# A table of PSUM banks, an output projection for two tiles, whole-tile turns and values, and another order of stages in the layers of a transformer kernel

## The chip, the core and the metric

The kernel runs on one core of a Trainium2 chip. Its engines work side by side, each through its own list of instructions in order: TensorE (PE; matmuls, with their weight loads as PEld), VectorE (DVE), ScalarE (ACT) and GpSimd (POOL); SyncE (SP) issues the DMAs. They wait for each other on semaphores. Matmul results land in PSUM, eight banks of 128 partitions x 512 float32 values; everything else lies in SBUF. The metric is the device time of one execution in microseconds (us), lower is better.

## What is computed

Two branches read the same normalised input of 2048 tokens x 128 features; their results and the input are added.

```python
xn = _layernorm(x)
x = x + _L0_attn_ref(xn, ...) + _L0_ffn_ref(xn, ...)

# dense attention: 16 heads of 8, softmax over all 2048 tokens, values, output projection
# the layers, DEPTH = 6, HEADS = 16, DIM_HEAD = 64, WINDOW = 32:
for i in range(DEPTH):
    x = attn_layer(shift_tokens(x), Wqkv[i], q_scale[i], k_scale[i], Wo[i]) + x
    x = ffn_layer(shift_tokens(x), ln_g[i], ln_b[i], W1[i], b1[i], W2[i], b2[i]) + x

def attn_layer(x, Wqkv, qs, ksc, Wo):
    q, k, v = heads of x @ Wqkv
    q, k = l2norm(q) * qs, l2norm(k) * ksc
    q, k = rotary of both: t * cos * scale + rotate_half(t) * sin * scale
    out = local_attention(q, k, v)      # windows of 32 see themselves and the 32 before
    return out @ Wo

def ffn_layer(x, g, bln, W1, b1, W2, b2):
    xn = layer norm of x, * g + bln
    a, gate = split(xn @ W1 + b1)
    return a * gelu(gate) @ W2 + b2
```

## The kernel before

The program has two stages. The first (functions ending in `_a`, about the first 800 us) does the dense attention; the change doesn't touch it. The second (ending in `_b`) does the six layers and ends with the sum of both branches.

The layers work on **tiles** of 128 tokens, 16 a layer, 96 in all, and on **chunks** of four tiles (512 tokens) for the MLP, 24 in all. Each engine has one loop `for u in range(FIRST, LAST)` in which it calls its stages, each for a tile or chunk that lies some steps back: `tile(u - 2)` is tile u-2 if there is one, `chunk(u - 5)` is a chunk in every fourth step only. The order of the calls in these loops is the order of the engine's instructions; it is written out by hand. A **step** here is one turn of the loop, one tile; four steps make a group with one chunk's MLP work.

The life of a tile: ScalarE rounds the input to its upper part (`high_x`), GpSimd makes the rest (`low_x`); TensorE projects q, k, v (`project`, six matmuls each into two banks); ScalarE squares q and k (`squares`), VectorE sums them (`square_sums`, `root_argument`), ScalarE takes logarithm, exponential and square (`root_estimate`), VectorE corrects the root (`root_slope`, `root_fix`) and scales (`normalise`). q is rotated by VectorE (`rotate_cos`, `rotate_sin`) and summed by GpSimd (`rotate_q_sum`); k is rotated and summed by GpSimd (`rotate_k_cos`, `rotate_k_sin`, `rotate_k_sum`). TensorE transposes both (`turn`), ScalarE evicts them (`turned_q`, `turned_k`, which also makes the 32 columns that the next tile sees). Then `score` on TensorE, `maxima` and `shifted` on VectorE, `exponentials` on ScalarE, `prob_sums` and `prob_reciprocals` on VectorE, `scale_probs` on GpSimd, `blocks` (a transposition in blocks of 32) on VectorE, `diagonals` (eight copies of 32 partitions) on ScalarE, `values` on TensorE, `values_out` on ScalarE, `output` on TensorE, `residual_1` on VectorE.

A chunk: `mean`, `deviation`, `deviation_squares`, `variance`, `add_epsilon`, `ln_root_estimate`, `first_scale`, `ln_root_slope`, `ln_root_fix`, `high_ln`, `scale_shift`, `low_ln`, three `up_product`s, three `gelu`s between two table loads of ScalarE, three `gated`, `down_product`, `residual_2`.

PSUM in the layers: `W_ps` is two pairs of banks for the projections and up products, `SB_ps` a pair for the scores, `T_ps` two single banks for all the rest. Who has which bank is counted in `bank_turns`: users take the two in turn, in the order of TensorE's list, so each waits until the last but one has been evicted. A tile's turn of q is four transposes into one `T_ps` bank and four into the other (halves `hf`), its values likewise; ScalarE evicts a half of 512 columns at a time.

```python
def turned_q(u, hf):
    w.wait_ge(s[f"turn0{hf}"], u + 1)
    w.wait_ge(s["score_mm"], u)
    e.activation(m.q_T[:, 4 * hf:4 * hf + 4, :], bank, ACT.Copy)...
```

## Time and profile before

| | us |
|---|---|
| median of 3 runs | 2631.66 (2623.95 to 2635.92) |
| the profiled execution | 2620.41 |
| its span, first to last instruction | 2618.6 |
| TensorE busy | 2284.9 (87%) |
| VectorE busy | 2249.0 (86%) |
| ScalarE busy | 2025.8 (77%) |
| GpSimd busy | 1327.1 (51%) |

The page says how long each engine was busy, in 40 slices of the span how busy it was, and it follows the chain of work that ended last: 40% TensorE, 29% VectorE, 24% ScalarE, 5% issue. In the dense stage (the first third) the chain is TensorE's almost alone; in the layers it changes engine every few instructions. The granted clock of TensorE is 0.952 of full speed in the mean. DMA carries 37 GB/s and is no limit. Below, a row of a timeline gives the start, the length and, in brackets, how long the engine was idle before it and who released it. Line numbers are those of the kernel before.

### The profile page before, as it was taken

To read this page: it belongs to the slowest core of one execution; us is meant where nothing else is said; L and a number is where in the kernel's file an instruction comes from. 1 tells how busy PE (TensorE), PEld (TensorE's weight loads), DVE (VectorE), ACT (ScalarE), POOL (GpSimd) and SP (SyncE) were. 2 spreads that over 40 slices of the span, in tenths; PEclk is the share of its full clock that TensorE was granted. 3 is DMA by queue.
4 is the path that set the end of the run, shared out by engine and by line. 5 is a ranking of instruction groups with operands and counts; after the bars stand their busy time and mean duration, and the time that the engine had idled before them with its cause. 6 is when DMAs were issued, how large, how long until landed. Compare 5 with 4: busy or idle time off the path is not lost.

```text
span 2618.6 us, 67512 instructions
## 1 busy us (share of the span) xinstructions
PE 2284.9 (87%) x28055; PEld 1393.2 (53%) x28151; DVE 2249.0 (86%) x2609; ACT 2025.8 (77%) x3616; POOL 1327.1 (51%) x894
## 2 busy tenths in 40 slices
PE   5899999999985898888988888888898998889886
PEld 3122222222213676666766666666676766666664
DVE  6999899999926889988889888888888888889984
ACT  1288787778873678888888888888888888888774
POOL 4111111101005567677676676677776666677660
PEclk8699999999997789999999999999999999999998
DMA  1212222222111100100011100101010000111000
GB/s 38 83 50 87 63 84 66 81 51 51 35 61 43 36 18 8 58 18 24 10 40 34 25 10 8 58 16 26 10 56 18 23 10 8 58 26 30 22 14 9
DMA packets 115173, 95.94 MB, mean 37 GB/s; under 512 B 72118, under 2 KB 89780, under 8 KB 114868
## 3 DMA queue, kind: packets, MB, share of 16 engines
q1 hardware_dynamic: 114516, 91.42, 12.7%
q8 instruction: 222, 3.64, 0.6%
q14 instruction: 83, 0.68, 0.1%
q10 hardware_dynamic: 352, 0.20, 0.0%
HBM read 57.83 MB, written 27.26 MB: 32 GB/s over the span
## 4 chain that ended last, share of the span: by engine, by line
PE 40%; DVE 29%; ACT 24%; issue 5%; POOL 1%; DMA 0%; ACTq 0%; DVEq 0%; SPq 0%; POOLq 0%
PE O_ps L1260 9%; PE E_ps L1252 8%; DVE ss L959 6%; PE S_ps L1243 5%; DVE mx L915 4%; ACT nrm L677 4%; DVE nrm L987 3%; ACT pT L746 3%; DVE mxB L1043 3%; PE W_ps L1284 3%; DVE tc L998 2%; PE T_ps L1402 2%; ACT pT L748 2%; PE W_ps L1286 2%; PE W_ps L1285 2%
## 5 line engine op out<-in xcount | busy, mean ns | idle before, releaser
L666 ACT ACTIVATE PT<-E_ps 128x512 f32<-128x512 f32 x1024 | 534.3, 602 | 186.8 <-PE E_ps L1252 185.1
L915 DVE TENSOR_REDUCE mx<-S_ps 128x1 f32<-128x1024 f32 x512 | 601.2, 1218 | 30.8 <-PE S_ps L1243 25.2
L1309 PE MATMUL T_ps<-ident,tc 128*128 128x128 f32 x1536 | 240.1, 289 | 174.1 <-ACT q_T L697 144.0
L608 POOL TENSOR_TENSOR tc<-tc,ts 128x1024 f32<-128x1024 f32 x96 | 228.2, 2377 | 289.5 <-DVE ts L1011 289.5
L1243 PE MATMUL S_ps<-KS,QS 48*128 48x512 bf16 x1024 | 326.8, 403 | 30.3 <-DVE mx L915 22.0
L1252 PE MATMUL E_ps<-QS,KS 64*128 64x512 bf16 x1024 | 318.0, 387 | 4.7 <-ACT PT L666 4.6
L543 POOL CAST w_cut_b<-w_raw_b 128x512 fp32r<-128x512 f32 (+1 forms) x48 | 27.6, 574 | 555.8 <-DMA w_raw_b<-in_Wqkv 417.1
L566 POOL TENSOR_TENSOR pr<-pr,mxB 128x1024 f32<-128x1024 f32 x96 | 182.7, 1903 | 223.8 <-DVE mxB L1050 223.8
L1309 PEld LDWEIGHTS T_ps<-ident,tc 128*128 128x128 f32 x1536 | 175.1, 145 | 221.4 <-ACT q_T L697 109.9
L1284 PE MATMUL W_ps<-w_qkv,x_cut 128*128 128x512 f32 x576 | 272.1, 472 | 23.6 <-issue 15.3
L959 DVE TENSOR_REDUCE ss<-nrm 128x16 f32<-128x1024 f32 x192 | 233.0, 1214 | 68.4 <-ACT nrm L677 66.6
L1260 PE MATMUL O_ps<-PT,va 128*32 128x512 f32 x2048 | 278.3, 616 | 0.0
L746 ACT ACTIVATE pT<-pc 32x512 f32<-32x512 f32 x384 | 240.0, 625 | 16.3 <-DVE pc L1023 9.6
L1252 PEld LDWEIGHTS E_ps<-QS,KS 64*128 64x128 bf16 x1024 | 78.8, 94 | 320.1 <-ACT PT L666 235.1
L677 ACT ACTIVATE nrm<-W_ps 128x1024 f32<-128x1024 f32 x192 | 193.1, 1006 | 58.7 <-PE W_ps L1286 58.7
L1323 PE MATMUL T_ps<-pT,v 128*64 128x128 f32 x3072 | 221.0, 288 | 19.1 <-ACT xl L817 6.4
L1285 PE MATMUL W_ps<-w_qkv,x_cut 128*128 128x512 f32 x576 | 235.2, 408 | 0.0
L1286 PE MATMUL W_ps<-w_qkv,x_cut 128*128 128x512 f32 x576 | 234.9, 408 | 0.0
L616 POOL TENSOR_TENSOR tc<-tc,ts 128x1024 f32<-128x1024 f32 x96 | 227.6, 2370 | 13.8
L588 POOL TENSOR_TENSOR tc<-nrm,rt 128x1024 f32<-128x1024 f32 x96 | 231.4, 2411 | 2.9 <-DVE nrm L987 2.9
L987 DVE TENSOR_TENSOR nrm<-W_ps,rs 128x1024 f32<-128x1024 f32 x192 | 221.9, 1197 | 0.1
L998 DVE TENSOR_TENSOR tc<-nrm,rt 128x1024 f32<-128x1024 f32 x96 | 210.3, 2191 | 0.0
(199 smaller groups left out, 4739.5 us busy)
## 6 DMA issues: line engine op xcount, KB each, us to landing
Wqkv_cut<-w_cut_b SPq DMA_DIRECT2D x72, 256.0 KB, 2.4
w_qkv<-Wqkv_cut SPq DMA_DIRECT2D x36, 512.0 KB, 4.7
rot<-in_rot SPq DMA_DIRECT2D x96, 128.0 KB, 2.5
w_raw_b<-in_Wqkv SPq DMA_DIRECT2D x36, 256.0 KB, 3.0
W_cut<-w_cut_b SPq DMA_DIRECT2D x24, 170.5 KB, 2.6
w<-W_cut SPq DMA_DIRECT2D x12, 341.0 KB
QS<-zp_q SPq DMA_DIRECT2D x96, 32.0 KB
w_o<-in_Wo SPq DMA_DIRECT2D x6, 512.0 KB, 4.0
```

The costliest lines, as they stand in the source:

```text
L666: e.activation(m.PT[n % NPT][:, :], turns.bank("probs", n)[:, :], ACT.Exp).then_inc(turns.sem("probs", n), 1)
L677: e.activation(m.nrms[u % 2][i][:, :].rearrange("p (a b) -> p a b", a=2), turns.w_bank("qk"[i], u)[:, :, :], ACT.Square).then_inc(s[f"sq{i ...
L746: e.activation(m.pT[r, :, r], m.pc[r, :, WIN:2 * WIN], ACT.Copy).then_inc(s["pD"], 1)
L915: e.tensor_reduce(m.mx[h % 2][:, i, hf:hf + 1], m.S_ps[n % 2][:, :, :], AX.XY, ALU.max).then_inc(s["sc_max"], 1)
L959: e.tensor_reduce(m.ss[u % 2][:, i * H:(i + 1) * H], view(m.nrms[u % 2][i][:, :]), AX.X, ALU.add).then_inc(s[f"ss{i}"], 1)
L987: e.tensor_tensor(view(m.nrms[u % 2][i][:, :]), bank[:, :, :].rearrange("p a (h d) -> p (a h) d", d=DH), m.rs[u % 2][2][:, i * H:(i + 1) * ...
L1243: mm = e.matmul(m.S_ps[n % 2][:, c, :], m.QS[sl][rows, i * P:(i + 1) * P], m.KS[sl][rows, k:k + CH], start=True, stop=True)
L1252: e.matmul(turns.bank("probs", n)[:, :], m.KS[sl][rows, j * P:(j + 1) * P], m.QS[sl][rows, chunk_cols(c)], start=True, stop=True).then_inc ...
L1260: e.matmul(m.O_ps[VC * c:VC * (c + 1), :], m.va[:, j, h, :], m.PT[n % NPT][:, :], start=(j == 0), stop=(j == NT - 1)).then_inc(s["pv"], 1)
L1284: e.matmul(bank, left[0], right[0], start=True, stop=False)
L1285: e.matmul(bank, left[0], right[1], start=False, stop=False)
L1309: t = e.transpose(bank[:, j, :], m.tcs[u % 2][i][:, b * P:(b + 1) * P], m.ident[:, :])
```

## The change

It touches the second stage alone.

- **Banks by a table.** PSUM is four pairs of banks, `ps[0]` to `ps[3]` (banks 0 to 7). `BANKS` gives each stage its bank or pair, for even and odd units. `bank_users` goes through TensorE's order and notes, for each use, the last user of each of its banks; `wait_free` waits for that user's eviction. The four counting semaphores `W_out`, `T_out` become one for each stage.
- **Whole tiles.** A turn is eight transposes into a pair of banks and one eviction of 1024 columns; so are the values. `turned_k` has one copy of 256 columns for the next tile in place of two of 128.
- **Output for two tiles.** `o_T` holds two tiles, `output` is eight matmuls of 256 columns in every second step, `residual_1` two additions of 256 columns.
- **The scores** alternate between two pairs of banks.
- **Order.** All five engines' loops are in another order and with other distances. In the diff `tile(u - 2)` for ScalarE stands for the tile that VectorE has at `u`.
- **Small.** `rotate_sin` no longer waits for `rotate_cos`; `squares` waits for `rotq_c`/`rotk_c` too; the buffers of the last addition are single; the weights of the next layer are loaded one tile later.

Of the loops of ScalarE, VectorE and TensorE the diff is shown without its removed lines, which stand in the kernel above.

```diff
-def bank_turns():
+BANKS = {"q": ((0, 1), (0, 1)), "k": ((2, 3), (2, 3)), "v": ((6, 7), (6, 7)),
+         "q_turn": ((6, 7), (6, 7)), "k_turn": ((4, 5), (4, 5)), "values": ((4, 5), (4, 5)),
+         "output": ((0,), (2,)), "score": ((6, 7), (4, 5)), "mean": ((6,), (6,)),
+         "var": ((2,), (2,)), "up0": ((4, 5), (4, 5)), "up1": ((2, 3), (2, 3)),
+         "up2": ((6, 7), (6, 7)), "down": ((5,), (3,)), "att": ((5,), (3,)),
...
+    def take(stage, unit):
         if unit is not None:
-            book[(name, unit) + rest] = len(book) + 1
+            of = BANKS[stage][unit % 2]
+            users[stage, unit] = [last[b] for b in of if b in last]
+            last.update({b: (stage, unit) for b in of})
...
+    def wait_free(self, w, stage, unit):
+        for had, n in self.m.users[stage, unit]:
+            w.wait_ge(self.s[OUT[had]], n + 1 - (CHUNKS - NC if had == "finish" else 0))
...
 def gpsimd_b(e, w, m, s):
...
     for u in range(FIRST, LAST):
-        scale_probs(tile(u - 4))
-        low_x(tile(u - 1))
-        rotate_k_cos(tile(u - 2))
-        rotate_q_sum(tile(u - 2))
-        rotate_k_sin(tile(u - 2))
-        rotate_k_sum(tile(u - 2))
         rotary(tile(u))
+        low_x(tile(u))
+        scale_probs(tile(u - 3))
+        rotate_k_cos(tile(u - 1))
+        rotate_q_sum(tile(u - 1))
+        rotate_k_sin(tile(u - 1))
+        rotate_k_sum(tile(u - 1))
...
 def scalar_b(e, w, m, s):
...
     for u in range(FIRST, LAST):
+        squares(tile(u - 2), 0)
+        squares(tile(u - 2), 1)
+        deviation_squares(chunk(u - 6))
+        high_ln(chunk(u - 7))
+        exponentials(tile(u - 4))
+        root_estimate(tile(u - 2))
+        values_out(tile(u - 5))
+        scale_shift(chunk(u - 7))
+        dense_output(early(u - 5))
+        turned_q(tile(u - 3))
+        turned_k(tile(u - 3))
         high_x(tile(u))
+        keep_v(tile(u - 2))
+        ln_root_estimate(chunk(u - 6))
+        gelu_table(chunk(u - 7))
+        gelu(chunk(u - 7), 0)
+        gelu(chunk(u - 7), 1)
+        diagonals(tile(u - 4), 3)
+        diagonals(tile(u - 4), 2)
+        diagonals(tile(u - 4), 1)
+        diagonals(tile(u - 4), 0)
+        gelu(chunk(u - 7), 2)
+        root_table(chunk(u - 7))
...
 def vector_b(e, w, m, s):
...
     for u in range(FIRST, LAST):
+        ln_root_fix(chunk(u - 5))
         maxima(tile(u - 2))
+        shifted(tile(u - 2))
         gated(chunk(u - 6), 2)
         square_sums(tile(u), 0)
+        deviation(chunk(u - 4))
         square_sums(tile(u), 1)
         root_argument(tile(u))
+        prob_sums(tile(u - 2))
+        low_ln(chunk(u - 5))
         root_slope(tile(u))
+        prob_reciprocals(tile(u - 2))
         root_fix(tile(u))
         normalise(tile(u), 1)
         dense_norm(early(u - 2))
+        normalise(tile(u), 0)
+        add_epsilon(chunk(u - 4))
+        blocks(tile(u - 2))
+        gated(chunk(u - 5), 0)
+        rotate_cos(tile(u))
+        first_scale(chunk(u - 4))
+        ln_root_slope(chunk(u - 4))
+        rotate_sin(tile(u))
+        final_add(late(u - 7))
+        residual_1(pair(u - 3))
+        gated(chunk(u - 5), 1)
+        residual_2(chunk(u - 6))
+        final_sum(late(u - 6))
...
 def tensor_b(e, w, m, s):
...
     for u in range(FIRST, LAST):
+        turn(tile(u - 2), 1)
         project(tile(u - 1), 2)
         up_product(chunk(u - 6), 0)
+        up_product(chunk(u - 6), 1)
+        down_product(chunk(u - 7))
         up_product(chunk(u - 6), 2)
+        finish(late(u - 8))
+        output(pair(u - 4))
+        variance(chunk(u - 5))
         score(tile(u - 2))
         project(tile(u), 0)
+        mean(chunk(u - 4))
         project(tile(u), 1)
+        values(tile(u - 3))
         dense_output(early(u - 3))
+        turn(tile(u - 1), 0)
```

Below, names are those of the tiles: `ss` is a sum of squares, `rs` the roots, `mxB` maxima, sums and reciprocals, `nrm` normalised q or k, `tc` and `ts` the cosine and sine products, `pc` the transposed blocks, `pr` the probabilities.

VectorE in a plain step, from the first `square_sums` to the sine product, before:

```order
L959 TENSOR_REDUCE ss<-nrm 128x16
L1043 TENSOR_REDUCE mxB<-pr 128x16
L959 TENSOR_REDUCE ss<-nrm 128x16
L966 TENSOR_SCALAR rs<-ss 128x32
L973 SCALAR_TENSOR_TENSOR rs<-rs 128x32
L980 SCALAR_TENSOR_TENSOR rs<-rs 128x32
L1050 RECIPROCAL mxB<-mxB 128x16
L987 TENSOR_TENSOR nrm<-W_ps,rs 128x1024 x2
L1023 STREAM_TRANSPOSE pc<-pr 128x1024
L998 TENSOR_TENSOR tc<-nrm,rt 128x1024
L1009 TENSOR_TENSOR ts<-nrm,rt 128x16x32
```

And after:

```order
L956 TENSOR_REDUCE ss<-nrm 128x16 x2
L963 TENSOR_SCALAR rs<-ss 128x32
L1037 TENSOR_REDUCE mxB<-pr 128x16
L970 SCALAR_TENSOR_TENSOR rs<-rs 128x32
L1044 RECIPROCAL mxB<-mxB 128x16
L977 SCALAR_TENSOR_TENSOR rs<-rs 128x32
L983 TENSOR_TENSOR nrm<-B_ps,rs 128x1024 x2
L1017 STREAM_TRANSPOSE pc<-pr 128x1024
L993 TENSOR_TENSOR tc<-nrm,rt 128x1024
L1003 TENSOR_TENSOR ts<-nrm,rt 128x16x32
L1005 TENSOR_TENSOR ts<-nrm,rt 128x16x32
```

The sums of the probabilities (`mxB<-pr`) moved from between the two sums of squares to behind `root_argument` (`rs<-ss`), the reciprocals before `root_fix`.

GpSimd in the same step, before, from `scale_probs` on (`pr<-pr,mxB`):

```order
L566 TENSOR_TENSOR pr<-pr,mxB 128x1024
L559 TENSOR_TENSOR x_cut<-stream,x_cut 128x128
L588 TENSOR_TENSOR tc<-nrm,rt 128x1024
L608 TENSOR_TENSOR tc<-tc,ts 128x1024
L598 TENSOR_TENSOR ts<-nrm,rt 128x16x32
L600 TENSOR_TENSOR ts<-nrm,rt 128x16x32
L616 TENSOR_TENSOR tc<-tc,ts 128x1024
L579 TENSOR_TENSOR rt<-rot,gains 128x256
```

And after:

```order
L565 TENSOR_TENSOR pr<-pr,mxB 128x1024
L586 TENSOR_TENSOR tc<-nrm,rt 128x1024
L606 TENSOR_TENSOR tc<-tc,ts 128x1024
L596 TENSOR_TENSOR ts<-nrm,rt 128x16x32
L598 TENSOR_TENSOR ts<-nrm,rt 128x16x32
L614 TENSOR_TENSOR tc<-tc,ts 128x1024
L578 TENSOR_TENSOR rt<-rot,gains 128x256
L558 TENSOR_TENSOR x_cut<-stream,x_cut 128x128
```

`low_x` (`x_cut`) moved from behind `scale_probs` to ahead of it; the rest of the row is as it was.

TensorE at the end of a step, before (turns are `ident,tc`, values `pT,v` and `pL,v`):

```order
L1309 MATMUL T_ps<-ident,tc 128x128 x4
L1323 MATMUL T_ps<-pT,v 64x128 x8
L1329 MATMUL T_ps<-pL,v 64x32 x8
L1309 MATMUL T_ps<-ident,tc 128x128 x4
L1323 MATMUL T_ps<-pT,v 64x128 x8
L1329 MATMUL T_ps<-pL,v 64x32 x8
L1309 MATMUL T_ps<-ident,tc 128x128 x8
```

And after, with the beginning of the next step:

```order
L1314 MATMUL B_ps<-pT,v 64x128 x16
L1320 MATMUL B_ps<-pL,v 64x32 x16
L1301 MATMUL B_ps<-ident,tc 128x128 x16
L1276 MATMUL B_ps<-w_qkv,x_cut 128x512
L1277 MATMUL B_ps<-w_qkv,x_cut 128x512
L1278 MATMUL B_ps<-w_qkv,x_cut 128x512
L1276 MATMUL B_ps<-w_qkv,x_cut 128x512
L1277 MATMUL B_ps<-w_qkv,x_cut 128x512
L1278 MATMUL B_ps<-w_qkv,x_cut 128x512
L1351 MATMUL B_ps<-o_T,w_o 128x256 x8
L1334 MATMUL B_ps<-mask_bf,ident_bf 128x512 x2
L1339 MATMUL B_ps<-k_T,q_T 32x64 x64
```

The values of a tile are in one piece, then q's turn, k's turn of the tile before it (together the row of 16), v's projection, the pair's output, the scores.

## Rows read from the trace of the kernel before

**Rows 1.** Busy times by stretch: start:end, length, engines (instructions), PEclk, DMA share, GB/s.

```profile
1600.00:2400.00 800.00, 709.90 (x10890) 547.90 (x10932) 702.83 (x869) 674.50 (x1177) 552.04 (x353) 0.97 0.10 27
```

**Rows 2.** `maxima` (L1029): its summary, then timeline rows of VectorE (start, us).

```profile
L1029 DVE TENSOR_REDUCE mxB<-SB_ps x96: 1214/1218/1226, 826.6 to 2565.8; 128x16 f32<-128x1024 f32 x96
...
1870.39 1.22 DVE L1029 TENSOR_REDUCE mxB<-SB_ps 128x16 f32<-128x1024 f32 x1
...
1886.50 1.22 DVE L1029 TENSOR_REDUCE mxB<-SB_ps 128x16 f32<-128x1024 f32 x1
...
1906.47 1.22 DVE L1029 TENSOR_REDUCE mxB<-SB_ps 128x16 f32<-128x1024 f32 x1
...
1924.92 1.22 DVE L1029 TENSOR_REDUCE mxB<-SB_ps 128x16 f32<-128x1024 f32 x1
```

**Rows 3.** Groups of instructions, 1600 to 2400 us: busy, mean ns | idle before, releasers.

```profile
L1309 PE MATMUL T_ps<-ident,tc 128*128 128x128 f32 x704 | 108.0, 286 | 76.9 <-ACT q_T L697 70.1 <-POOL tc L608 3.1 <-ACT o_T L719 3.1
```

**Rows 4.** Timeline of VectorE, one step, 1937 to 1951 us.

```profile
1937.99 2.51 DVE L998 TENSOR_TENSOR tc<-nrm,rt 128x1024 f32<-128x1024 f32 x1
1940.61 0.69 DVE L1009 TENSOR_TENSOR ts<-nrm,rt 128x512 f32<-128x512 f32 x1
...
1941.83 1.22 DVE L1029 TENSOR_REDUCE mxB<-SB_ps 128x16 f32<-128x1024 f32 x1
...
1948.38 1.01 DVE L966 TENSOR_SCALAR rs<-ss 128x32 f32<-128x32 f32 x1
1950.20 0.19 DVE L973 SCALAR_TENSOR_TENSOR rs<-rs 128x32 f32<-128x32 f32 x1 [0.82 <-ACT rs L689]
```

**Rows 5.** Timeline of GpSimd, the same step.

```profile
1934.77 1.90 POOL L566 TENSOR_TENSOR pr<-pr,mxB 128x1024 f32<-128x1024 f32 x1 [1.63 <-DVE mxB L1050]
...
1937.05 2.38 POOL L588 TENSOR_TENSOR tc<-nrm,rt 128x1024 f32<-128x1024 f32 x1
1941.99 2.40 POOL L608 TENSOR_TENSOR tc<-tc,ts 128x1024 f32<-128x1024 f32 x1 [2.56 <-DVE ts L1011]
...
1946.99 2.36 POOL L616 TENSOR_TENSOR tc<-tc,ts 128x1024 f32<-128x1024 f32 x1
...
1950.86 1.90 POOL L566 TENSOR_TENSOR pr<-pr,mxB 128x1024 f32<-128x1024 f32 x1 [0.83 <-DVE mxB L1050]
```

**Rows 6.** Groups of instructions, 1600 to 2400 us, ScalarE and VectorE.

```profile
L746 ACT ACTIVATE pT<-pc 32x512 f32<-32x512 f32 x176 | 110.0, 625 | 3.1
...
L697 ACT ACTIVATE q_T<-T_ps 128x512 f32<-128x512 f32 x88 | 51.2, 582 | 0.0
...
L734 ACT ACTIVATE v<-W_ps 128x1024 f32<-128x1024 f32 x44 | 45.2, 1028 | 18.1 <-PE W_ps L1286 17.7
...
L810 ACT ACTIVATE gel<-W_ps,b 128x512 f32<-128x512 f32 x22 | 15.1, 687 | 6.0 <-PE W_ps L1286 5.9
L795 ACT ACT_TABLE_LOAD x11 | 14.1, 1283 | 0.2
...
L791 ACT ACTIVATE xl<-xl,cols 128x512 f32<-128x512 f32 x11 | 8.8, 803 | 0.0
...
L1079 DVE TENSOR_SCALAR lnv<-T_ps 128x512 f32<-128x512 f32 x11 | 7.6, 692 | 2.9 <-PE T_ps L1381 2.4
```

**Rows 7.** Timelines of TensorE, then ScalarE, 1934 to 1940 us.

```profile
1934.71 1.07 PE L1309 MATMUL T_ps<-ident,tc 128*128 128x128 f32 x8 [0.41 <-ACT q_T L697]
1935.85 0.50 PE L1284 MATMUL W_ps<-w_qkv,x_cut 128*128 128x512 f32 x1
...
1939.30 2.05 PE L1364 MATMUL T_ps<-o_T,w_o 128*128 128x128 f32 x16
...
1937.55 1.02 ACT L734 ACTIVATE v<-W_ps 128x1024 f32<-128x1024 f32 x1 [0.38 <-PE W_ps L1286]
```

**Rows 8.** TensorE's timeline at 1602 us, then busy times and clock at 1604 us.

```profile
1602.20 0.66 PE L1309 MATMUL T_ps<-ident,tc 128*128 128x128 f32 x4 [1.89 <-ACT q_T L697]
...
1604.00:1605.00 1.00, 1.00 (x18) 0.93 (x16) 1.00 (x4) 0.81 (x1) 0.56 (x1) 0.50 0.00 0
```

441 lines of the change are left out of this document (183 added, 258 removed).

## The prediction

> **What bounds the kernel now.** I read four views, in this order. The busy times of a long stretch of the layers say that no engine is full: in 800 us TensorE is busy 710, VectorE 703, ScalarE 675, GpSimd 552 [rows 1]. So a dependency cycle sets the step, not one engine's sum. The rows of `maxima` give the step: 96 of them between 826.6 and 2565.8 us, 95 steps at 18.31 us; a regular group of four steps takes 16.11, 19.97, 18.45 and 16.91, together 71.44 us (17.86 a step) [rows 2]. The difference, 0.45 us a step or 43 us in all, is what disturbed groups cost.
>
> Among the waits the change speaks to one: in these 800 us TensorE's turns wait 70.1 us for the eviction of q_T [rows 3]. But the timelines of one step show who ends last. VectorE works back to back from one `maxima` to the next, but for the 0.82 us in which `root_slope` waits for ScalarE's roots, and for two instructions that are long without having more work: the cosine product took 2.51 us and ended as GpSimd's cosine product of k (1937.05 + 2.38) was over plus about 1.1, and the tiny `root_argument` took 1.01 us and ended with GpSimd's sum of k (1946.99 + 2.36 = 1949.35) [rows 4, 5]. An instruction of VectorE that reads only SBUF thus stands still while a GpSimd instruction runs. I call this the lock. GpSimd in turn waits 2.56 us for the sine product and 0.83 us for the reciprocals [rows 5]. VectorE and GpSimd hold each other in one cycle; TensorE's wait for an eviction, 1.89 us at its longest here [rows 8], lies beside it.
>
> The Trainium skill, GPSIMD Engine Reference, section 1 (Specifications), says that GpSimd shares its SBUF interfaces with VectorE and contends with VectorE instructions in a 2-port mode or with two SBUF inputs. It gives no price and doesn't say that the one waits for the other's end; if contention only slowed the two a little, the new step would be the 15.2 us of the first rival.
>
> **ScalarE and TensorE, the visible part.** Two evictions of 512 columns (2 x 0.582) become one of 1024 (1.028 in the nearest row, v) [rows 6]: 0.14 less for each of q_T, k_T and o_T. The two carry copies of 128 columns become one of 256; between nothing and 0.58 less (the 512-column eviction is the upper bound), I take 0.3. Together 0.7 us a tile of ScalarE. The output product has the same columns in half the instructions: 16 passes of 128 columns take 2.05 us [rows 7], a pair's 16 passes of 256 should take 3.5 to 4.1, so between 0.1 more and 0.3 less a tile. The turns no longer wait for each other's banks, which frees up to 70.1/44 = 1.6 us a step of TensorE. None of this is on the cycle of VectorE and GpSimd. Cost or gain on the path: nothing, as long as the path through them stays shorter than the new step. It is: roots 0.82, eviction of o_T 1.03, then k's turn and v's projection up to v's eviction (1937.55 - 1934.71 = 2.84), x_cut and v 1.3 (between one and two evictions; x_cut is 128 columns), eight copies of 0.625 = 5.0, two squares of 1.0 each, a sum of 1.2, some 0.3 of handoffs: 14.5 us [rows 4, 6, 7].
>
> **The plain step.** Take the start of GpSimd's `scale_probs` as zero. Before, the sum of k ended at 1949.35 - 1934.77 = 14.58 [rows 5]. In the new order `low_x` no longer stands between `scale_probs` and the cosine product of k (1937.05 - 1934.77 - 1.90 = 0.38 less), and the removed wait of the sine product on the cosine product frees 0.11 (1937.99 + 2.51 to 1940.61) [rows 4, 5]: 14.1. VectorE gets there: the normalisations and the block transposition end at 3.5, the cosine product must wait for the lock till 4.3 and ends as before. Next, `root_argument`. It is ready 14.5 us after the last one, that is 1.2 us before the step is over, and GpSimd's sum of k has then been running since 11.7: it waits for the lock until 14.1. Then come the sums of the probabilities (moved between argument and slope, 1.2 us, which hides the 0.82 us of roots), slope 0.1 and reciprocals 0.3: the next `scale_probs` starts at **15.7**. GpSimd itself would be ready at 14.1 + 0.7 (`rotary`, from 1949.35 to 1950.86 - 0.83) + 0.4 (`low_x`) = 15.2. So the gain of hiding the roots is eaten by the sums put in their place.
>
> **The three steps with the MLP's work.** Times again from `scale_probs`, in the order of tiles 2 to 5 of a group.
> - Into the step with `deviation`: TensorE has the pair's output product (3.5) and, new, the two passes of `mean` (half of the 2.05 in rows 7, since the columns are) ahead of k's projection. Squares and sum come 1.0 us later each, `root_argument` is ready at 14.9, just behind the sum of k, and is held by `low_x` till 15.1: 15.1 + 1.7 = **16.8** (before 16.1).
> - With `add_epsilon`: it waits for the variance product, which stands behind k's turn and v's projection (about 3.9 instead of 2.3); blocks 1.2, cosine 1.1, two operations of 0.6 and the sines 1.2 bring q's sine to 9.3 instead of 6.7, and `ln_root_fix` may go ahead of GpSimd's sum in the lock (0 to 0.69, I take 0.5). The sum of k, 7.4 behind q's sine as in the plain step, ends at 17.2. Then `low_ln`, now ahead of `root_slope`, waits for ScalarE's roots 0.8, o_T 0.9 and `scale_shift` 0.8, which the same `root_argument` held, and takes 0.6 (each to the start of the next, 0.1 less than its length); with slope and reciprocals 17.2 + 0.8 + 0.9 + 0.8 + 0.6 + 0.4 = **20.7** [rows 6] (before 20.0).
> - With the gelus: ScalarE has two table loads of 1.28, three gelus of 0.69; TensorE has, in a row from 1.6 before zero, k's turn 1.1, six products of v 1.4 (1.70 up to the eviction that follows, so 0.24 each), 18 up products 4.3, the pair's output 3.5, the score 2.0 (to 1939.30), q 1.4 and k 1.7, with 0.4 of waits for a bank 15.8 [rows 7]. k is projected at 14.3, squares and sum follow: `root_argument` at 16.7, **18.4** (before 18.5).
> - The fourth is plain, 15.7; `down` and `residual_2` fall into VectorE's wait for the lock (before 16.9, where they stood on its full cycle).
>
> Sum 15.7 + 16.8 + 20.7 + 18.4 = **71.6 us** against 71.4. Over 95/4 = 23.75 groups: +4 us. The disturbed groups' 43 us I leave as they are. The end of the program gains nothing to overlap: the pair's product and the whole evictions are on its chain, about +3 us. Loads move by a tile on SP, each with over a step of slack; at nothing. The profiled execution took 2620.4 us (span 2618.6) and would become 2627; the median of the runs lies 11.3 above it: **2639 us**, no change within 0.5% (13 us, about what a measurement of this kernel can tell).
>
> **The rivals.**
> 1. *The lock does not hold `root_argument`.* It arrives only a little after GpSimd's sum of k has begun; ScalarE 0.7 us faster than I think and it slips in before. Then GpSimd's own work is the bound: 15.2 in the plain step; in that of `add_epsilon` the argument goes at 15.1 instead of 17.2, of which `low_ln` loses 0.7 again in the lock to `rotary`: 20.7 - 2.1 + 0.7 = 19.3; the others as they are: 69.7 a group, 1.9 x 23.75 = 45 us less, 2594. For it: in the plain step it is ready at 12.8 and the sum of k began at 11.7, a margin of 1.1 us out of a sum of twelve terms. Against it: terms that I left out make it later, not earlier, and a delay on TensorE does too.
> 2. *The order does more than I see.* `low_ln` finds its operand ready (17.2 + 1.7 = 18.9), `mean` costs nothing (15.7), the plain step runs at 15.2: with 18.4 it is 68.2 a group, 3.4 x 23.75 = 81 us less, 2558. TensorE's own work, 710/11 = 64.5 a group [rows 1], is not yet reached then.
> 3. *TensorE's clock, on the slower side.* Before, a wait of 1.89 us on TensorE (at 1602) was followed by a granted clock of 0.50, that is 1.2 instead of 2.4 GHz [rows 8], for about 7 us. The new order gathers TensorE's idle time: between the end of q's turn and k's turn 2 us in plain steps, 2.4 and 2.9 in the `add_epsilon` step, directly ahead of the gelu step, in which TensorE sets the path. It decides as soon as the fall comes in every group: 7 us at half speed is 3.5 us late, 83 us in all instead of the 43 that are in the sum, so 2679. For it: longer waits than those that lowered the clock before. Against it: a slow TensorE fills its own gaps, and most waits of 1.9 us before were followed by nothing.
> 4. *It doesn't do what it says* (the banks still collide, an eviction of 1024 costs two of 512): 0.4 us a tile on ScalarE, which has 1.2 us of slack; that is inside the forecast.
>
> **How the numbers follow.** Forecast 0.37 (2625 to 2655), rival 1 0.25, rival 2 0.10, rival 3 0.28. Within 0.5% of 2631.7 lie two thirds of the forecast: 0.25. Faster: rivals 1 and 2 and a little of the forecast, 0.39; slower: rival 3 and the rest, 0.36. The range reaches from rival 2 to a little above rival 3, 2560 to 2695; the forecast's own is 2625 to 2655.
>
> **What would show it.** In the new trace: `root_argument` of 1 to 2.4 us that ends with GpSimd's sum of k (right), or of 0.18 everywhere and a plain step of 15.2 (rival 1). Steps between `maxima` of about 15.7, 16.8, 20.7, 18.4. TensorE's waits for q_T gone, the waits for diagonals and k's turn in their place. GpSimd's wait for the sine product near 2.5 in plain steps. A granted clock of 0.5 in every group (rival 3). I am wrong if the plain step is under 15 us: then the cycle isn't the one I took.

## The result, and the profile after

The kernel after takes 2612.17 us in the median (4 runs, 2608.35 to 2616.07) against 2632.54 of before (now 4 runs, 2623.95 to 2635.92), a ratio of 0.9928 with a 95% interval of 0.9899 to 0.9956. It is 20 us faster; I had forecast 2639, no change. The page of after has less of VectorE (2249.0 before) and ScalarE (2025.8), the same TensorE, and TensorE has 55% of the chain in place of 40:

```profile
PE 2285.1 (88%) x27383; PEld 1414.2 (54%) x27383; DVE 2189.6 (84%) x2513; ACT 2010.7 (77%) x3232; POOL 1330.3 (51%) x894
...
PE 55%; DVE 24%; ACT 14%; issue 6%; POOL 0%; DMA 0%; ACTq 0%; DVEq 0%; SPq 0%; POOLq 0%
```

Of `maxima`, compare [rows 2], first the summary of all 96 (their times in ns, the first and the last start), then five timeline rows of VectorE over one regular group (start, length, and in brackets the idle time before it with its releaser):

```profile
L1023 DVE TENSOR_REDUCE mxB<-B_ps x96: 1216/1224/1227, 825.4 to 2550.2; 128x16 f32<-128x1024 f32 x96
```

And the five rows:

```profile
1911.15 1.22 DVE L1023 TENSOR_REDUCE mxB<-B_ps 128x16 f32<-128x1024 f32 x1
...
1926.85 1.23 DVE L1023 TENSOR_REDUCE mxB<-B_ps 128x16 f32<-128x1024 f32 x1 [0.87 <-PE B_ps L1339]
...
1944.50 1.22 DVE L1023 TENSOR_REDUCE mxB<-B_ps 128x16 f32<-128x1024 f32 x1
...
1967.69 1.22 DVE L1023 TENSOR_REDUCE mxB<-B_ps 128x16 f32<-128x1024 f32 x1 [0.20 <-PE B_ps L1339]
...
1982.85 1.23 DVE L1023 TENSOR_REDUCE mxB<-B_ps 128x16 f32<-128x1024 f32 x1
```

The steps are 15.70, 17.65, 23.19 and 15.2 us, together 71.7. Over all the regular groups of this trace the sum is 71.65 (15.16 + 15.71 + 17.65 + 23.13). Before had 71.44. So the regular group, for which my sum said 71.6, did not get shorter. The 95 steps still shrank from 1739.2 to 1724.8 us, and I split that as the prediction did: 23.75 groups x 71.44 = 1696.7 and 42.5 of disturbance before; 23.75 x 71.65 = 1701.7 and 23.1 after. The regular groups are 5 us dearer (forecast: 4), **the disturbance is 19.4 us cheaper (forecast: 0)**. Most of it lies in the middle of the layers, where six groups of before took 73.0 to 74.9 us, 16.7 us too much in all, and after has at most 0.6 us too much in a group; the first two groups are 6 us less disturbed than before, the last three 5 us more. Outside, the layers start 1.2 us earlier and the end, from the last `maxima` on, is 56.4 us in place of 52.8, 3.6 more (forecast: 3).

That is 12 us of the profiled execution; the medians differ by 20, since before's profiled execution lay 12 us under its median and after's 4 (2608.35). The disturbance differs from one execution to the next: in 18 runs of before beside the first experiments the time went from 2615 to 2647. That these runs were longer by more disturbed groups is a reading, since only one execution of each kernel has a trace.

**What I had called the lock** is where it was forecast. Timelines of GpSimd and VectorE, of the plain step and of the step of `add_epsilon`:

```profile
1914.78 2.36 POOL L614 TENSOR_TENSOR tc<-tc,ts 128x1024 f32<-128x1024 f32 x1
...
1916.03 1.15 DVE L963 TENSOR_SCALAR rs<-ss 128x32 f32<-128x32 f32 x1
...
1949.43 2.35 POOL L614 TENSOR_TENSOR tc<-tc,ts 128x1024 f32<-128x1024 f32 x1
...
1950.07 1.75 DVE L963 TENSOR_SCALAR rs<-ss 128x32 f32<-128x32 f32 x1
```

`root_argument` (L963) takes 1.15 and 1.75 us in place of 0.18, and each time ends with GpSimd's sum of k (1914.78 + 2.36 = 1917.14; 1949.43 + 2.35 = 1951.78). In the plain step the forecast was a hold of 1.3 us (12.8 to 14.1); it is 1.0.

**TensorE's clock** is what I had as rival 3, and it came. Below, a fall is a stretch in which the granted clock is 0.50, 1.2 in place of 2.4 GHz. Timelines of TensorE and ScalarE, of a group at 1875 us:

```profile
1874.89 2.64 PE L1314 MATMUL B_ps<-pT,v 128*64 128x128 f32 x32 [2.45 <-ACT pL L747]
...
1883.54 0.78 PE L1276 MATMUL B_ps<-w_qkv,x_cut 128*128 128x512 f32 x1
...
1889.00 1.27 ACT L811 ACTIVATE gel<-B_ps,b 128x512 f32<-128x512 f32 x2
```

Two 1-us windows there; behind the five engines' busy times stands the granted clock:

```profile
1874.00:1875.00 1.00, 0.11 (x2) 0.11 (x4) 0.97 (x2) 0.95 (x3) 1.00 (x1) 1.00 0.00 0
1878.00:1879.00 1.00, 1.00 (x24) 1.00 (x22) 0.89 (x2) 0.44 (x1) 1.00 (x1) 0.50 0.00 0
```

TensorE waited 2.45 us for the last diagonal, because ScalarE makes the diagonals behind `ln_root_estimate` in this step, and from 1876 on the clock was 0.50 for 10.2 us. Regular groups of before had no such fall; after has one of 3.4 to 10.2 us in nearly every group, each in this step. Summed over 1-us windows from 780 us on, that is 287 us at half clock against 162. The group at 2054 us was an exception: the fall ended early, v's projection ran at full clock:

```profile
2098.57 0.50 PE L1276 MATMUL B_ps<-w_qkv,x_cut 128*128 128x512 f32 x1 [0.46 <-ACT q_T L700]
...
2102.81 1.27 ACT L811 ACTIVATE gel<-B_ps,b 128x512 f32<-128x512 f32 x2
```

From `scale_probs` to the first gelu it took 4.13 us (2098.68 to 2102.81), in the group above 5.43 (1883.57 to 1889.00), and the step was 21.93 instead of 23.1. So this fall costs 1.2 us, wherever v's projection is still inside it.

### The profile page after: what moved, and what is told of

Read it like the earlier page. It is cut to its first block, busy times and chain, and to the rows that moved or that the text cites. A ratio compares the mean times of both kernels' runs of the same rounds, so it can differ in the third digit from the quotient of the medians.

```text
span 2606.6 us, 65283 instructions
## 1 busy us (share of the span) xinstructions
PE 2285.1 (88%) x27383; PEld 1414.2 (54%) x27383; DVE 2189.6 (84%) x2513; ACT 2010.7 (77%) x3232; POOL 1330.3 (51%) x894
## 4 chain that ended last, share of the span: by engine, by line
PE 55%; DVE 24%; ACT 14%; issue 6%; POOL 0%; DMA 0%; ACTq 0%; DVEq 0%; SPq 0%; POOLq 0%
PE O_ps L1252 9%; PE E_ps L1244 8%; DVE ss L956 7%; PE B_ps L1351 6%; PE B_ps L1276 5%; PE S_ps L1235 5%; PE B_ps L1277 4%; PE B_ps L1278 4%; PE B_ps L1301 4%; DVE mx L912 4%; PE B_ps L1339 3%; ACT o_T L721 3%; DVE rs L963 3%; ACT nrm L680 2%; ACT pT L745 2%
## 5 line engine op out<-in xcount | busy, mean ns | idle before, releaser
L606 POOL TENSOR_TENSOR tc<-tc,ts 128x1024 f32<-128x1024 f32 x96 | 236.1, 2459 | 355.6 <-DVE ts L1005 355.6
L1235 PE MATMUL S_ps<-KS,QS 48*128 48x512 bf16 x1024 | 326.7, 403 | 30.2 <-DVE mx L912 21.9
L1301 PE MATMUL B_ps<-ident,tc 128*128 128x128 f32 x1536 | 241.7, 309 | 103.5 <-ACT o_T L721 94.7
L1276 PE MATMUL B_ps<-w_qkv,x_cut 128*128 128x512 f32 x576 | 271.8, 472 | 24.9 <-issue 15.4
L1301 PEld LDWEIGHTS B_ps<-ident,tc 128*128 128x128 f32 x1536 | 194.7, 159 | 134.3 <-issue 121.8
L1314 PE MATMUL B_ps<-pT,v 128*64 128x128 f32 x3072 | 205.6, 291 | 62.2 <-ACT pL L747 59.4
L680 ACT ACTIVATE nrm<-B_ps 128x1024 f32<-128x1024 f32 x192 | 193.6, 1025 | 82.8 <-PE B_ps L1278 80.3
L1278 PE MATMUL B_ps<-w_qkv,x_cut 128*128 128x512 f32 x576 | 240.7, 418 | 1.8 <-issue 1.8
L1277 PE MATMUL B_ps<-w_qkv,x_cut 128*128 128x512 f32 x576 | 241.0, 418 | 0.0
L614 POOL TENSOR_TENSOR tc<-tc,ts 128x1024 f32<-128x1024 f32 x96 | 227.8, 2373 | 13.8
L1314 PEld LDWEIGHTS B_ps<-pT,v 128*64 128x64 f32 x3072 | 179.7, 145 | 99.4 <-ACT pL L747 70.5
L983 DVE TENSOR_TENSOR nrm<-B_ps,rs 128x1024 f32<-128x1024 f32 x192 | 226.6, 1220 | 3.3
```

Of the source, the lines that this page charges most:

```text
L1235: mm = e.matmul(m.S_ps[n % 2][:, c, :], m.QS[sl][rows, i * P:(i + 1) * P], m.KS[sl][rows, k:k + CH], start=True, stop=True)
L1276: e.matmul(bank, left[0], right[0], start=True, stop=False)
L1277: e.matmul(bank, left[0], right[1], start=False, stop=False)
L1278: return e.matmul(bank, left[1], right[0], start=False, stop=True)
L1301: t = e.transpose(bank[:, b, :], m.tcs[u % 2][i][:, b * P:(b + 1) * P], m.ident[:, :])
L1314: mm = e.matmul(bank[at, j, :], m.v[u % NV][:, p * DH:(p + 1) * DH], m.pT[:, h, :], start=(j % 4 == 0), stop=(u % NT == 0), skip_group_che ...
```

## Where before lost part of its 42 us

Three neighbouring groups of before, from 1559 us on, took 74.8, 74.9 and 73.0 us in place of 71.44, three more did so from 1996 us. These six are 16.7 of the 42.5 us; the first two groups of the layers are 16.8, the last two 7.5. Timelines of TensorE and VectorE in the first:

```profile
1585.19 1.06 PE L1309 MATMUL T_ps<-ident,tc 128*128 128x128 f32 x8 [1.22 <-ACT q_T L697]
1586.76 2.07 PE L1373 MATMUL T_ps<-stream,ones 128*128 128x512 f32 x2 [0.51 <-ACT k_T L710]
...
1588.87 0.69 DVE L1071 TENSOR_TENSOR xl<-stream,T_ps 128x512 f32<-128x512 f32 x1 [1.47 <-PE T_ps L1373]
...
1602.20 0.66 PE L1309 MATMUL T_ps<-ident,tc 128*128 128x128 f32 x4 [1.89 <-ACT q_T L697]
```

And the 1-us window at 1588:

```profile
1588.00:1589.00 1.00, 1.00 (x2) 0.45 (x2) 0.13 (x1) 0.00 (x0) 1.00 (x1) 0.50 0.00 0
```

k's turn waits 1.22 us for the eviction of q_T and the `mean` 0.51 for that of k_T; then the clock falls to 0.50 for 3.4 us, right under the `mean`, which takes 2.07 us; the deviation waits 1.47 for it; 13 us later q's second turn finds its bank taken for 1.89 us, and the clock falls again, for 6.8 us. The group costs 3.4 us more, and the next one has the same waits again. The regular groups have the same two waits, 1.19 to 1.23 us and 0.51, without a fall. One of them, TensorE's timeline:

```profile
1950.80 1.06 PE L1309 MATMUL T_ps<-ident,tc 128*128 128x128 f32 x8 [1.19 <-ACT q_T L697]
1952.37 1.12 PE L1373 MATMUL T_ps<-stream,ones 128*128 128x512 f32 x2 [0.51 <-ACT k_T L710]
```

So the same waits are followed by a fall in some groups and by none in others; that one fall brings the next is a reading of the row of three, not shown by a run. Both waits are for T_ps banks, which the change took away. No run here has the table of banks without the new order, so which of the two parts ended the disturbed groups is not separated. In their place the turns wait for o_T, 50.4 us in 1600 to 2400 us where it was 70.1 for q_T [rows 3]; the group of instructions in after (busy, mean ns, idle before, releaser):

```profile
L1301 PE MATMUL B_ps<-ident,tc 128*128 128x128 f32 x704 | 107.2, 301 | 50.4 <-ACT o_T L721 50.4
```

**Experiment e3_clock_before** makes TensorE busy in the first of the two waits, in the kernel before, and does nothing else; `filler(u, n)` is n products of `mask_bf` with `ident_bf`, 512 columns each, into SB_ps once its last scores are read:

```diff
+        filler(tile(u - 2), 5 if chunk(u - 4) is not None else 0)
         turn(tile(u - 1), 1, 1)
```

> The kernel before, with five more products of 512 bf16 columns on TensorE ahead of k's turn in the step of the mean, where TensorE waits 1.2 us for the eviction of q_T; they write into the scores' banks, which the next scores overwrite. In the trace of before the regular groups (71.44 us) have no fall of the clock, and the groups of 73.0 to 74.9 us begin with a granted clock of 0.50 for 3.4 us right behind this wait. Theory A (the disturbed groups are the clock's): they go away, and with them 17 us of the profiled execution's 1559 to 2219 us; before's median of 2632 falls to 2605 to 2615, that is to the time of after, ratio 0.990 to 0.994. Theory B (something else disturbs these groups, and the fall of the clock follows from it): the groups of 74.8 us stay, ratio 1.000, or 1.002 for the added work.

Measured: 2610.26 us (10 runs, 2598.40 to 2614.33), ratio 0.9933 [0.9909, 0.9957]. It is the time of after. (Each ratio is to the kernel before as it ran beside that experiment, 2626.6 or 2630.75 us in the median where the result had 2632.54; differences to after are given below in us of the medians, and by the ratios they come out up to 5 us otherwise.) The groups from 1559 us on, `maxima` on VectorE's timeline of this kernel:

```profile
1560.09 1.22 DVE L1029 TENSOR_REDUCE mxB<-SB_ps 128x16 f32<-128x1024 f32 x1
...
1631.53 1.22 DVE L1029 TENSOR_REDUCE mxB<-SB_ps 128x16 f32<-128x1024 f32 x1
...
1702.97 1.22 DVE L1029 TENSOR_REDUCE mxB<-SB_ps 128x16 f32<-128x1024 f32 x1
```

71.4 us each; of the six disturbed groups none is left. Single falls of 3.4 us, at the wait of 1.89 us for q_T, remain in one group of four (72.4 us). At the beginning of the layers two groups are 3.8 us shorter in sum, at the end two are 3.2 longer. Theory A holds: the six disturbed groups were the clock's, and taking them away is worth what the whole change is worth.

**Experiment e2_clock_after** does the same in the kernel after, at its two long waits, into the banks of the stage that it names:

```diff
+        filler("values", tile(u - 3), 8 if chunk(u - 5) is not None else 0)
         values(tile(u - 3))
...
+        filler("q_turn", tile(u - 1), 8 if chunk(u - 5) is not None else 0)
         turn(tile(u - 1), 0)
```

> The kernel after, with sixteen more products of 512 bf16 columns on TensorE in each group, eight between k's projection and the values and eight between the values and q's turn in the step of the variance, where the trace of after shows TensorE waiting 2.45 us for the diagonals and up to 3.03 us for the eviction of o_T, followed by a granted clock of 0.50 for 10.2 us in nearly every group. They write into banks that the next products overwrite; nothing reads them. Theory A (the fall of the clock costs what v's projection takes longer ahead of the first gelu, 2.6 in place of 1.35 us): the step that ends with the gelus goes from 23.1 to 21.9 us, as in the one group at 2054 us whose v projection ran at full clock, -1.2 x 23.75 = -29 us, about 2583. Theory B (what follows the fall is set by the lock and ScalarE, and TensorE at half speed only fills its own gaps): 0, or +0.5 us a group for the added work: 2612 to 2624.

Measured: 2593.71 us (2590.71 to 2602.76), ratio 0.9875 [0.9840, 0.9910]; 18 us less than after (14 by the ratios), not 29. Two `maxima` around the step of the gelus:

```profile
1866.83 1.21 DVE L1023 TENSOR_REDUCE mxB<-B_ps 128x16 f32<-128x1024 f32 x1
...
1888.72 1.23 DVE L1023 TENSOR_REDUCE mxB<-B_ps 128x16 f32<-128x1024 f32 x1 [0.20 <-PE B_ps L1339]
```

In 15 of 19 regular groups it is 21.9 us, in ten the whole group is 70.4 to 70.7. In the others a fall of 3.4 us came at another place, at a wait of 1.3 to 1.6 us of k's turn for o_T, and cost 1.2 to 1.6. The mean is 71.2. Theory A is right for the step and gave too much for the kernel: a filler moves the edge, it does not take away what makes TensorE wait.

## Is it the lock that holds the roots?

**Experiment e1_no_argument** takes `root_argument` from VectorE in the kernel after (`root_slope` then reads `m.ss` too; `m.tiny` holds 1e-24):

```diff
-        w.wait_ge(s["rB_arg"], u + 1)
-        e.activation(r[1][:, :], r[0][:, :], ACT.Ln).then_inc(s["rB_ln"], 1)
+        w.wait_ge(s["ss0"], u + 1)
+        w.wait_ge(s["ss1"], u + 1)
+        w.wait_ge(s["zeroB"], 4)
+        e.activation(r[1][:, :], m.ss[u % 2][:, :], ACT.Ln, bias=m.tiny[:, 0:1]).then_inc(s["rB_ln"], 1)
...
-        root_argument(tile(u))
```

> The kernel after, with root_argument (the small instruction of VectorE that in the trace of after takes 1.15 us in the plain step and 1.75 us in the step of add_epsilon, because it stands still until GpSimd's sum of k is over, in place of 0.18) taken from VectorE: ScalarE's logarithm reads the sums of squares themselves and adds 1e-24 as its bias. Theory A (the lock holds the roots, and through them the eviction of o_T, k's turn and the whole gelu step): in the step of add_epsilon the roots, o_T, scale_shift and low_ln all come 1.7 us earlier; in the plain step root_slope, which also reads only SBUF, now waits for the end of the sum of k, so only 0.45 us are left there (GpSimd's own work, 15.0 us, is then the bound); 0.3 us in the other two. Sum about -2.4 us of a group's 71.65, times 23.75: -57 us, about 2555, 0.970 of before. Theory B (TensorE, slowed by its clock, or ScalarE sets the group, and the lock lies beside it): at most the 0.45 us of the plain step, -10 us, about 2602.

Measured: 2529.73 us (2525.35 to 2536.06), ratio 0.9630 [0.9596, 0.9665]: 82 us less than after, where A had said 57. The regular steps are 14.9, 14.8, 17.4 and mostly 20.2 to 21.6, the group 68.2 in the mean. The step of the gelus gains more than I summed. The clock gained beside it: k's turn in that step now waits 1.33 us in place of up to 3.03, falls are 3.4 or 6.8 us but for one of 10.2, and two of the 19 regular groups have none. How much of the gain is the clock's is not separated here; e5, below, has both edits.

**Experiment e10_argument_as_sum** leaves the instruction where it is and changes its kind:

```diff
-        e.tensor_scalar(m.rs[u % 2][0][:, :], m.ss[u % 2][:, :], 1e-24, None, ALU.max).then_inc(s["rB_arg"], 1)
+        e.tensor_reduce(m.rs[u % 2][0][:, :], m.ss[u % 2][:, :].unsqueeze(2), AX.X, ALU.add).then_inc(s["rB_arg"], 1)
```

> The kernel after with root_argument as a reduction over one element each (it leaves out the maximum with 1e-24): the same number of instructions, the same places, waits and operands in SBUF, another kind of instruction. In all traces so far VectorE's reductions keep their length beside GpSimd, while its two-operand and scalar instructions that read only SBUF stand still. If that is the lock, this reduction takes 0.1 to 0.2 us everywhere in place of 1.15 and 1.75, the step of add_epsilon and the gelus get what taking root_argument away gave less 0.15 us a step: 2540 to 2550, 0.968 to 0.970. If root_argument was long for another reason (its place, its wait for two semaphores, its handoff to ScalarE), it stays long: 2612.

Measured: 2532.30 us (2525.43 to 2540.39), ratio 0.9641 [0.9603, 0.9679]: 80 us less than after. The summary of this line (min/median/max in ns) in the kernel after:

```profile
L963 DVE TENSOR_SCALAR rs<-ss x96: 181/316/1752, 803.1 to 2516.8; 128x32 f32<-128x32 f32 x96
```

And in e10:

```profile
L963 DVE TENSOR_REDUCE rs<-ss x96: 185/186/191, 792.6 to 2436.0; 128x32 f32<-128x32 f32 x96
```

Up to 1752 ns as a scalar operation, never over 191 as a reduction, in the same place with the same waits and operands. This is the sharpest of the runs: neither the place nor the handoff made it long. It also narrows what the prediction had said, that an instruction of VectorE that reads only SBUF stands still beside GpSimd: the reduction reads only SBUF and does not. The Trainium skill, SBUF — State Buffer, section "Who interferes with whom", states that the pair of ports shared by VectorE and GpSimd is given out as an exclusive lock, that `tensor_scalar` can take it and that `tensor_reduce` never does on this chip; by that rule, the two rows agree.

**Experiment e7_before_no_argument** is the same edit as e1 in the kernel before.

> The kernel before with root_argument off VectorE in the same way (the logarithm reads the sums of squares, 1e-24 as its bias). In the trace of before root_argument takes 0.18, 1.01, 0.61 and 0.18 us in the four steps of a regular group. Lock theory: in the step with 1.01 root_slope now goes at the end of GpSimd's sum of k, 0.85 us earlier; 0.2 in the one with 0.61, where ScalarE is busy until then; 0.1 in the others: 71.44 becomes 70.2, -30 us, 2600, 0.988. It is less than the kernel after gains by the same edit (3.3 us a group), since before has TensorE's way to the scores shorter (v's projection and k's turn don't wait for the roots of the next tile). If the gain of that edit is only the instruction itself and its handoffs (0.1 to 0.2 us a step), both kernels gain the same: 0.6 us a group, -14 us.

Measured: 2611.46 us (2600.66 to 2618.33), ratio 0.9931 [0.9911, 0.9951]: 15 to 18 us less, not 30. The steps without a fall are close to what was expected (16.75, 15.57, 19.71, 18.32; 70.35 us, expected 70.2), but in 19 of 20 regular groups there is one. TensorE's timeline in one:

```profile
1174.32 1.09 PE L1312 MATMUL T_ps<-ident,tc 128*128 128x128 f32 x4 [1.90 <-ACT q_T L701]
```

The 1-us window behind it:

```profile
1175.00:1176.00 1.00, 1.00 (x8) 0.67 (x9) 1.00 (x3) 0.97 (x3) 0.04 (x1) 0.50 0.00 0
```

q's second turn now waits 1.90 us for the T_ps bank that q_T's first half is evicted from, and a fall of 3.4 or 6.8 us follows; the step goes from 19.71 to 20.5 to 21.9. The mean of the regular groups is 71.7: per group the falls take 1.3 us, more than the 1.1 that the lock gave against 71.44, and what is left of the gain is that the groups of 73 to 75 us are gone. The number alone would have fitted the rival (the instruction only, -14 us); the steps of the trace speak against it: the four are shorter by 0.15, 0.55, 0.26 and 0.13 us, where the instruction alone would give 0.1 to 0.2 in each.

**Experiment e12_before_both** adds fillers to that kernel, five as in e3 and six ahead of q's second turn.

> The kernel before without root_argument on VectorE and with added products on TensorE ahead of its two longest waits for q_T (five in the step of the mean, six in the next). In the kernel before without root_argument nearly every group has a fall of the clock of 3.4 or 6.8 us, each right behind a wait of 1.90 us of q's second turn for the eviction of q_T; the step with it takes 20.5 to 21.9 us, the one without 19.7. Without falls: 16.75 + 15.57 + 19.71 + 18.32 = 70.35 us a group, 2585, 0.984. Set against the kernel after with both edits (67.2 us a group, 2513) it says what order, banks and whole tiles are worth once lock and clock are out of the way: 3.1 us a group, 70 us. If the added products don't prevent the falls: 2611.

Measured: 2607.23 us (2601.04 to 2611.00), ratio 0.9918 [0.9886, 0.9949], 22 us over what was expected. The falls at the two filled waits are gone, but the fillers stand in TensorE's way (15.84 and 20.18 in place of 15.57 and 19.71, 0.7 us a group), and in seven of the 20 regular groups a fall of 3.4 or 6.8 us comes in the step of the gelus, at another wait for q_T, of 1.57 us. It costs 0.7 to 0.9 us there, and 0.5 to 1.6 us in the step behind it.

**Experiment e5_both** has the edits of e1 and e2 (with five fillers ahead of q's turn) in the kernel after.

> Both changes to the kernel after together: root_argument off VectorE, and the added products of TensorE (eight ahead of the values, five ahead of q's turn, once a group). Without root_argument the groups still have falls of the clock: with none the step of the gelus takes 20.15 us, with 3.4 us at 0.50 it takes 20.6 to 21.2, with 6.8 us 21.5; the mean of the regular groups is 68.2 us. If the two causes are separate (lock and clock), every group becomes one without a fall, 14.8 + 17.4 + 20.2 + 14.9 = 67.2 us, -1.0 x 23.75 = -24 us: 2506, 0.954 of before. If the earlier roots already took away what the clock could cost, nothing is left: 2530, or above it by the added work.

Measured: 2513.31 us (2510.97 to 2516.58), ratio 0.9569 [0.9542, 0.9597], the fastest version of this study. One group of `maxima`:

```profile
1850.41 1.23 DVE L1027 TENSOR_REDUCE mxB<-B_ps 128x16 f32<-128x1024 f32 x1
...
1865.13 1.22 DVE L1027 TENSOR_REDUCE mxB<-B_ps 128x16 f32<-128x1024 f32 x1 [0.33 <-PE B_ps L1342]
...
1882.49 1.21 DVE L1027 TENSOR_REDUCE mxB<-B_ps 128x16 f32<-128x1024 f32 x1
...
1902.71 1.23 DVE L1027 TENSOR_REDUCE mxB<-B_ps 128x16 f32<-128x1024 f32 x1 [0.20 <-PE B_ps L1342]
...
1917.78 1.23 DVE L1027 TENSOR_REDUCE mxB<-B_ps 128x16 f32<-128x1024 f32 x1
```

14.72, 17.36, 20.22 and 15.07 us; nearly all regular groups are 67.1 to 67.5, as expected. Set beside e12, the same two kinds of edit on before, it says what order, banks and whole tiles are worth once the held `root_argument` and most falls are out of the way. The times give 2607 - 2513 = 94 us, but e12 has fillers that don't fit and falls that e5 hasn't; from the steps without either, 70.35 against 67.2 us a group, it is 3.15 x 23.75 = 75 us. In the change as it stands this is covered: the new order has `root_argument` held in two steps a group, by 1.0 and 1.6 us, and its idle time in one piece, which lowers the clock.

## The terms of the sum, one by one

**Experiment e4_low_ln_late** moves `low_ln` off the way to `scale_probs`.

```diff
-        low_ln(chunk(u - 5))
         root_slope(tile(u))
         prob_reciprocals(tile(u - 2))
         root_fix(tile(u))
+        low_ln(chunk(u - 5))
```

> The kernel after, with low_ln moved from ahead of root_slope to behind root_fix. In the trace of after VectorE waits 1.31 us for scale_shift and then takes 0.69 us for low_ln, and with it root_slope, the reciprocals and GpSimd's scale_probs wait. The prediction had these 1.9 us on the path (0.8 + 0.9 + 0.8 + 0.6 after the sum of k, in the step of 20.7). Theory P (the prediction: the cycle of VectorE and GpSimd sets this step): -1.9 us a group, -45 us, about 2567. Theory T (the next step is TensorE's: eviction of o_T, k's turn, v's projection, the up products, the output product, the scores, and scale_probs only waits for nothing in it): the step before gets 1.9 us shorter and the gelu step 1.9 us longer, sum unchanged, 2612.

Measured: 2608.95 us (2603.60 to 2617.75), ratio 0.9930 [0.9908, 0.9952], the time of after. GpSimd's `scale_probs` in this kernel, around the step of `add_epsilon` and that of the gelus:

```profile
1869.12 1.91 POOL L565 TENSOR_TENSOR pr<-pr,mxB 128x1024 f32<-128x1024 f32 x1 [1.11 <-DVE mxB L1044]
...
1887.54 1.90 POOL L565 TENSOR_TENSOR pr<-pr,mxB 128x1024 f32<-128x1024 f32 x1 [0.43 <-DVE mxB L1044]
...
1909.07 1.90 POOL L565 TENSOR_TENSOR pr<-pr,mxB 128x1024 f32<-128x1024 f32 x1 [1.75 <-DVE mxB L1044]
```

18.42 and 21.53 us, where after has 20.4 and 19.6: two us shorter, then two us longer. My sum put `low_ln` on the path because it counted from one `scale_probs` to the next. It is on VectorE's way there, but the next step begins with TensorE's k turn, which waits for o_T and not for `scale_probs`.

**Experiment e8_low_x_back** undoes one move on GpSimd:

```diff
-        low_x(tile(u))
         scale_probs(tile(u - 3))
+        low_x(tile(u))
```

> The kernel after with GpSimd's low_x behind scale_probs again (0.45 us, ahead of the cosine product of k). In the two steps in which VectorE's cosine product is held until GpSimd's cosine product of k is over (1.89 us in the trace of after), sine products, sum of q and sum of k come 0.45 us later; in the plain step root_argument is held by that sum, so the step is 0.4 us longer; in the step of the deviation root_argument is held only 0.1 us, so it is 0.2 to 0.4 us longer; in the other two VectorE's cosine product is free, 0. Sum +0.6 to +0.8 us a group, +14 to +19 us, 2627 to 2631. The prediction had this term as 0.38 in the plain step. Rival (GpSimd has slack everywhere, its order doesn't matter): 0, 2612.

Measured: 2640.97 us (2636.16 to 2643.69), ratio 1.0052 [1.0036, 1.0068], 29 us over after. Two steps are longer by 0.41 us each (15.57 and 18.06, where after has 15.16 and 17.65), the cosine products being held that much longer; and in every second group a fall of 3.4 us comes in the first step, 1.6 us more there; in front of it k's turn waits 2.05 us for o_T, where in after it waits 1.62. The first part is what I had expected (14 to 19 us), the second brings the rest.

**Experiment e6_halves** undoes what whole tiles bring to ScalarE; each of these three in two, and the carry:

```diff
-        e.activation(m.q_T[:, :, :], bank, ACT.Copy).then_inc(s["qT_out"], 1)
+        e.activation(m.q_T[:, 0:4, :], bank[:, 0:4, :], ACT.Copy)
+        e.activation(m.q_T[:, 4:8, :], bank[:, 4:8, :], ACT.Copy).then_inc(s["qT_out"], 1)
```

> The kernel after with ScalarE evicting q_T, k_T and o_T (1.01 us each in the trace of after) in two instructions of 512 columns each, as before (0.58 each), and the copy of 256 columns (0.47) as two of 128. This undoes what whole tiles bring to ScalarE, 4 x 0.15 to 0.3 = 0.6 to 0.7 us a tile; turns, banks and order stay. Prediction's term (evictions are not on the path): 0, 2612. Other reading, of the trace of after: in the step of add_epsilon k's turn waits for o_T, v's projection waits for q_T, and both are on TensorE's way to the next scores: 0.15 + 0.15 us a group, and what the longer wait adds to the fall of the clock, at most 0.5: +7 to +19 us, 2619 to 2631.

Measured: 2609.36 us (2604.26 to 2617.06), ratio 0.9933 [0.9912, 0.9955]; no difference. One step is 15.82 in place of 15.71, the rest is the same. The prediction's zero was right: ScalarE's 0.7 us a tile are saved off the path.

**Experiment e9_sums_back** undoes the moves of the sums and of the reciprocals on VectorE:

```diff
         square_sums(tile(u), 0)
         deviation(chunk(u - 4))
+        prob_sums(tile(u - 2))
         square_sums(tile(u), 1)
         root_argument(tile(u))
-        prob_sums(tile(u - 2))
         low_ln(chunk(u - 5))
         root_slope(tile(u))
-        prob_reciprocals(tile(u - 2))
         root_fix(tile(u))
+        prob_reciprocals(tile(u - 2))
```

> The kernel after with prob_sums between the two square_sums again and the reciprocals behind root_fix, as before; all else stays as in after, also ScalarE's exponentials behind both squares. The prediction says that hiding the 0.82 us of the roots behind the sums is worth nothing net, since the sums themselves then stand in their place: 0, 2612. From the trace of after: the exponentials end only when the second square is long ready, so the sums hold up the second square_sums, root_argument and the roots: +0.5 us in the plain step (where the lock covers the rest), +2.0 in the step of the deviation, +0.7 in that of add_epsilon, +1.2 to +1.9 in that of the gelus; 4.4 to 5.1 us a group, +105 to +121 us, 2717 to 2733.

Measured: 2848.18 us (2838.76 to 2850.04), ratio 1.0835 [1.0795, 1.0874]: 236 us over after, twice what I had expected and far from the prediction's zero. VectorE and TensorE in the step of the deviation:

```profile
1928.68 1.22 DVE L1037 TENSOR_REDUCE mxB<-pr 128x16 f32<-128x1024 f32 x1 [1.90 <-ACT pr L728]
...
1933.16 1.94 PE L1301 MATMUL B_ps<-ident,tc 128*128 128x128 f32 x8 [3.06 <-ACT o_T L721]
```

VectorE waits 1.90 us for the exponentials with the second sum of squares behind it; the roots, o_T and k's turn come later by as much, TensorE waits 3.06 us for o_T, and now the clock falls in all four steps of a group (20 us at 0.50 in one group of 82). Of the parts that were undone one at a time, this is by far the dearest; with it undone, as with `low_x` (e8), the kernel is slower than before.

**Experiment e13_output_behind_k** tries to shorten the longest step of e5.

```diff
         project(tile(u), 1)
+        output(pair(u - 4) if u % 4 == 1 else None)
```

> The kernel after with both edits (no root_argument, added products), and with the pair's output product of the step of the gelus moved from ahead of the scores to behind k's projection (bank 6 in place of 0), its addition from behind the sines to behind root_fix. In the trace of after with both edits that step is TensorE's way: k's turn, v, 18 up products, output 3.6 us, scores, maxima; 20.15 us between maxima, where the others take 14.8 to 17.4. Without the 3.6 us ahead of the scores the bound becomes ScalarE with its eight copies, two table loads and three gelus: I expect 17.5 to 18.5 in place of 20.15, -2.2 us a group, -50 us: 2460, 0.937. If the product is missed where it now stands (q's turn waits for its addition): 2513 or more.

Measured: 2547.71 us (2542.94 to 2558.47), ratio 0.9692 [0.9651, 0.9733], 34 us over e5. The step of the gelus became 17.6 us, inside what was expected, and the next one 18.6 to 18.8 in place of 14.9; the end, from the last `maxima` on, is 63.3 us in place of 53.5. TensorE's timeline there:

```profile
1932.75 3.72 PE L1356 MATMUL B_ps<-o_T,w_o 128*128 128x256 f32 x16 [1.53 <-DVE hid L1115]
```

The product waits 1.53 us for its bank (until `gated` has read the last up product) and then stands, with 3.7 us, ahead of values, k's turn, `down_product` and the next scores. The work moved from one step in which TensorE is the path into the next, and made that one so.

## Why the prediction was wrong

| step, from one `scale_probs` to the next (us) | forecast | after | groups without a fall (e2) |
|---|---|---|---|
| plain | 15.7 | 15.5 | 15.5 |
| into `deviation` | 16.8 | 16.2 | 16.2 |
| `add_epsilon` | 20.7 | 20.4 | 20.4 |
| gelus | 18.4 | 19.6 | 18.3 |
| group | 71.6 | 71.7 | 70.4 |

The column of after comes from GpSimd's timeline:

```profile
1903.16 1.91 POOL L565 TENSOR_TENSOR pr<-pr,mxB 128x1024 f32<-128x1024 f32 x1 [1.79 <-DVE mxB L1044]
...
1918.67 1.90 POOL L565 TENSOR_TENSOR pr<-pr,mxB 128x1024 f32<-128x1024 f32 x1 [0.44 <-DVE mxB L1044]
...
1934.88 1.91 POOL L565 TENSOR_TENSOR pr<-pr,mxB 128x1024 f32<-128x1024 f32 x1 [1.11 <-DVE mxB L1044]
...
1955.29 1.90 POOL L565 TENSOR_TENSOR pr<-pr,mxB 128x1024 f32<-128x1024 f32 x1 [2.42 <-DVE mxB L1044]
...
1974.85 1.91 POOL L565 TENSOR_TENSOR pr<-pr,mxB 128x1024 f32<-128x1024 f32 x1 [1.77 <-DVE mxB L1044]
```

- **The step that failed** is "the disturbed groups' 43 us I leave as they are". I had shown their first cause myself, the wait of 1.89 us for q_T at 1602 us [rows 8], and had said that the change removes such waits; I drew the consequence for the busy path alone (nothing) and not for the clock. In the profiled executions the 42.5 us became 23.1, and the six groups of the middle make 16.7 of that; e3, which ends these six by added products alone, takes 16 us less than before, about what the change takes.
- **Regular groups: right in sum, by two errors that cancel.** Without falls the group would be 70.4, 1.2 less than my 71.6. Half of it is the step into `deviation` (16.2 for 16.8): I had `root_argument` ready at 14.9 and held until 15.1; it started 14.4 us after `scale_probs` (1933.08 - 1918.67), beside nothing but a rest of 0.1. The fall of the clock in nearly every group then gave 1.2 back, in the step of the gelus, which at full clock is the 18.4 of the forecast to 0.1.
- **Rival 3** had the right mechanism, a fall in every group ahead of the gelus, and the wrong price: it put 3.5 us on each fall, 83 us in all in place of the old 43, and 2679. Here a fall in this step costs 1.2 us, and 1.2 x 23.75 is 28.5 us; e2 got 14 to 18 of them back.
- **Rival 1** (the lock doesn't hold `root_argument`) did not come, and e1 and e10 priced it: 75 to 82 us, where I had 45. The cycle of VectorE and GpSimd is not all that hangs on the roots; o_T's eviction, k's turn and the clock do too, on the other side.
- **Evictions, banks, output for two tiles: nothing on the path**: right (e6). The tail: 3 forecast, 3.6 measured.
- **"The gain of hiding the roots is eaten by the sums put in their place"**: right as arithmetic of the plain step, wrong as a statement on the move. Seen from the new order of ScalarE it avoids 10 us a group (e9).
- **`low_ln` on the path**: in the sum to the next `scale_probs` yes, in the group no (e4).

What stays open: which part of the change ended the disturbed groups; what starts a disturbed row of three groups in before, where the same waits pass without a fall in most groups; and why after's last groups (75 to 78 us) and the first two (75 and 79) are long, beyond that each has falls.

## What to carry to other kernels

A steady loop with some groups disturbed has two times, and a change can act on the second alone: sum both, and ask of each disturbed group what triggers it and whether the change touches that. Where the granted clock falls at waits of 1.2 to 2.5 us, as here, the waits that matter are those of TensorE, even when nothing on the path waits for them; a few products into a bank that is overwritten anyway cost less than the fall, if they fit the gap (e2, e3; in e12 they didn't). And a small VectorE instruction on SBUF that stands beside GpSimd's long ones is worth rewriting as a reduction, or giving to ScalarE: here about 80 us of 2612 for one line.

## What the runs showed of the hardware that I had not expected

- At one and the same size the kind of a VectorE instruction decides whether it is held: 128x32 as `tensor_scalar` up to 1.75 us, as `tensor_reduce` 0.19 (e10).
- Falls of the clock in the regular groups of after lasted 3.4, 6.8 or 10.2 us, and their length hardly matters here: the step of the gelus takes 23.1 to 23.2 us with 10.2 us at half clock as with 3.4 (the groups at 1839 and 1911 us), since both cover v's projection.
- TensorE sometimes stands still without waiting for anything that the profile shows, "issue". Twice in e5's regular groups, for 1.66 and 4.26 us, it was followed by a fall, and these are its two long groups (69.2 and 71.7 us). One of them, TensorE's timeline:

```profile
2152.27 0.35 PE L1342 MATMUL B_ps<-k_T,q_T 64*32 64x64 f32 x16 [4.26 <-issue]
```

It is 4.26 us within the scores of one tile. No experiment here was about it.
